# Attention in a macaron block: weighted sums turned and divided by VectorE in 32x32 blocks, and a new place for every job of the loop

## The chip, the cores and the metric

One core of a Trainium2 chip. The metric is the device time of one execution of the whole kernel in microseconds, the median of several runs. One execution was also taken by the hardware profiler; every row below is from it.

## What is computed

The input x holds 32 sequences of 256 tokens of width 128. Three residual steps follow one another:

```python
x = x + 0.5 * ffn(layernorm(x))      # shared SwiGLU + top-2 of 8 experts
x = x + attn(layernorm(x))           # causal, 16 heads of width 8
x = x + 0.5 * ffn(layernorm(x))      # the same weights again

def attn(x, W_Q, W_K, W_V, W_O):     # shapes: [32, 256, 128]
    Q, K, V = x @ W_Q.T, x @ W_K.T, x @ W_V.T      # split into 16 heads of 8
    s = where(causal, Q @ K.T / sqrt(8), -inf)
    return (softmax(s) @ V) @ W_O.T
```

The change touches the attention step alone.

## The kernel before, in words

x lies in SBUF all the time, as 64 tiles of 128 tokens. The three steps are three phases, `ffn_phase`, `attention_phase`, `ffn_phase`; each is one block in which the engines run their own instruction lists in order and meet by semaphores. Products with the weights are made of three 16-bit products (high by high, low by high, high by low), so an activation is split into a high half (a float16 copy, ScalarE) and a low half (the value minus the high half, VectorE).

`attention_phase` goes over 16 chunks of 512 tokens (two sequences, b = 0 and 1). A **turn** of the loop handles one chunk in eight **units** (b, j), j = 0 to 3; unit 0 is (0, 0), unit 4 is (1, 0). A unit is four of the 16 heads, one in each group of 32 rows. In a unit

- TensorE makes, interleaved (`both`, L1011), the key-major scores of this unit (`head_t`, L998, into three `prob` banks) and the first two of three parts of the query-major scores of the unit five ahead (`score_head`, L966, behind a causal mask that is added by a product, L956, into two `score` banks in turn). Then come the jobs of place 0, the weighing of V by the exponentials of the unit before (`weigh`, L1038, into the `o` bank), the third part of the query-major scores, and the jobs of places 1 and 2.
- VectorE takes the maxima of the three score parts (`maxima`, L1136): parts 0 and 1, then the jobs of place 0, then part 2, then the jobs of places 1 and 2. TensorE may begin a score part when the part two before it has its maximum.
- ScalarE takes the three exponentials (L1214), then the jobs of place 0, then copies the o bank of the unit before to SBUF (`take_o`, L1220), then the jobs of places 1 and 2.
- GpSimd zeroes the two causal triangles in the exponentials (L1256).

A **job** is any smaller step that passes through one of two `job` banks, which the jobs take in turn, in the order of the table PLACES (L747). TensorE writes the bank; ScalarE or VectorE or both take it; a job may begin when the one two before it has been taken. The jobs: x (turn the normalised chunk, L882; high half L1186, low half L1094), q and k (projections, L889; high halves L1189 in two halves of the rows, low halves L1098), Q00 to Q11 and K00 to K11 (place the heads for the row groups, L899; packed by VectorE at L1103 or ScalarE at L1193, L1197), v (L905, L1200), m00 to m11 (turn the negated maxima, L937; added into q's pack at L1108), o00 to o11 (turn the copied sums, L913; reciprocal L1113 and product L1115), y0 and y1 (turn y back, L922; high half L1204, low half L1121) and z0 and z1 (product with W_O; added to x at L1124). SHIFT (L754) tells for which chunk, ahead or behind, a job is done in a turn. The scores of a sequence wait for its packs Q and K of the second half (L946), the key-major products for its m jobs (L984).

The layer norm for the next chunks is spread over VectorE and GpSimd: `norm_stats` and `norm_moments` (L76, L85) at unit 5, `norm_root` on GpSimd, and `norm_scale` (L110) on VectorE at unit 6. In the feed-forward phase the scaling is done on ScalarE (L609), with `norm_shift` on GpSimd before it.

The o bank holds for each of the four groups a block of 32 rows: 8 rows of the sum, one row of the divisor (from a column of ones in `v_ones`) and 23 of zeros, over 256 queries.

Ahead of the loop one list of jobs, the maxima of the first sequence, the jobs m00, m01, x, z0, and the first maxima of the second sequence are done; behind it the last weighing and the jobs that are left.

Of the kernel before, what the change touches and what calls it, by code (L numbers as in the profile page):

```python
# [5 lines left out]
ALU = mybir.AluOpType  # L6
# [6 lines left out]
P = 128  # L13
# [12 lines left out]
MAX_ROW = 3 * HEAD  # L26
SCALE = float(HEAD) ** -0.5
# [34 lines left out]
LN_STEPS = 2 * TILES  # L62

# [654 lines left out]
def select_heads(nc, consts, done):  # L718
# [35 lines left out]
SHIFT = {n: -2 if n == "x" else -1 if n in ("m00", "m01") or n[0] in "qkQKv" else 1 if n in ("o10", "o11", "y1", "z1")  # L754
         else 0 for n in JOBS}
# [22 lines left out]
def attention_phase(nc, x, consts, w, norms):  # L778

    with ExitStack() as ctx:  # L780
# [6 lines left out]
        def sem(name):  # L787
# [19 lines left out]
        o_t = [sb(f"o_t{s}", [P, UNITS, SEQ], F32) for s in range(2)]  # L807
        inv = sb("inv", [P, 2, UNITS, GROUPS], F32)
        y = sb("y", [P, 2, P], F32)
# [10 lines left out]
        xhi_done, qkhi_done, yhi_done, inv_done = (sem(n) for n in ("xhi_done", "qkhi_done", "yhi_done", "inv_done"))  # L820
        mask_begun = sem("mask_begun")
        scored, max_done = sem("scored"), sem("max_done")
        st_done, exp_done, masked, pv_done, o_done = (
            sem(n) for n in ("st_done", "exp_done", "masked", "pv_done", "o_done"))
# [35 lines left out]
        def _(pe):  # L860
# [14 lines left out]
            def job(c, slot, name):  # L875
# [31 lines left out]
                elif kind == "o":  # L907

                    b, t = int(name[1]), int(name[2])
                    pe.wait_ge(o_done, c * 2 * UNITS + (b + 1) * UNITS)  # L910
                    dst, done = begin(c, name)
                    for j in range(UNITS):
                        last = nc.tensor.transpose(dst[:, j * P:(j + 1) * P], o_t[b][:, j, t * P:(t + 1) * P],  # L913
                                                   ident[:, :])
                elif kind == "y":
                    b = int(name[1])

                    wait_taken(pe, c, f"o{b}0")
                    wait_taken(pe, c, f"o{b}1")
                    dst, done = begin(c, name)  # L920
                    for t in range(2):
                        last = nc.tensor.transpose(dst[:, t * P:(t + 1) * P], y[:, t, :], ident[:, :])  # L922
                elif kind == "z":

                    wait_taken(pe, c, "y" + name[1])
# [100 lines left out]
            def weigh(c, slot, b, j):  # L1026
# [47 lines left out]
        def _(dve):  # L1074
# [7 lines left out]
            def scale(c):  # L1082

                wait_taken(dve, c - 1, "x")
                norm_scale(dve, nc, norm0 + c, chunk_rows(x, c), buf, ln_rooted, ln_done)

            def job(c, slot, name):
                kind = name[0]
                if kind in "Kv" or (kind == "Q" and name[2] == "1"):
                    return  # L1090
# [9 lines left out]
                elif kind == "Q":  # L1100

                    wait_count(dve, st_done, (c - 1) * 6 * UNITS)
                    last = nc.vector.tensor_copy(packed(q_pack[slot], name),  # L1103
                                                 src[:, :].rearrange("p (g n) -> p g n", n=SEQ))
# [4 lines left out]
                elif kind == "o":  # L1109

                    b, t = int(name[1]), int(name[2])
                    o = src[:, :].rearrange("p (j g r) -> p j g r", j=UNITS, r=ROWS)
                    nc.vector.reciprocal(inv[:, t, :, :], o[:, :, :, HEAD]).then_inc(inv_done, 1)  # L1113
                    dve.wait_ge(inv_done, c * 4 + 2 * b + t + 1)
                    last = nc.vector.tensor_tensor(y[:, t, :].rearrange("p (g j d) -> p j g d", j=UNITS, d=HEAD),  # L1115
                                                   o[:, :, :, 0:HEAD],
                                                   inv[:, t, :, :].unsqueeze(3).to_broadcast([P, UNITS, GROUPS, HEAD]),
                                                   ALU.mult)
                elif kind == "y":
                    dve.wait_ge(yhi_done, c * 2 + int(name[1]) + 1)  # L1120
# [222 lines left out]
```

## Time and profile before

| | us |
|---|---|
| median of 3 runs | 1214.66 |
| lowest and highest | 1207.71, 1216.27 |
| the profiled execution | 1208.36 |
| its span | 1205.8 |
| TensorE busy (matmul) | 1106.7, 92% |
| VectorE busy | 1001.9, 83% |
| ScalarE busy | 789.6, 65% |
| GpSimd busy | 562.8, 47% |

The span is from the first to the last instruction of the profiled execution. PE is TensorE's matmul, PEld its weight load, DVE VectorE, ACT ScalarE, POOL GpSimd. Busy shares are means over stages with different limits, and a matmul's duration is modelled, so it overlaps the next one's.

### The profile page before, as it was taken

To read this page: it belongs to the slowest core of one execution; us is meant where nothing else is said; L and a number is where in the kernel's file an instruction comes from. 1 tells how busy PE (TensorE), PEld (TensorE's weight loads), DVE (VectorE), ACT (ScalarE), POOL (GpSimd) and SP (SyncE) were. 2 spreads that over 40 slices of the span, in tenths; PEclk is the share of its full clock that TensorE was granted. 3 is DMA by queue.
4 is the path that set the end of the run, shared out by engine and by line. 5 is a ranking of instruction groups with operands and counts; after the bars stand their busy time and mean duration, and the time that the engine had idled before them with its cause. 6 is when DMAs were issued, how large, how long until landed. Compare 5 with 4: busy or idle time off the path is not lost. (4 is left out here: it accounts for less than half of the span.)

```text
span 1205.8 us, 31981 instructions
## 1 busy us (share of the span) xinstructions
PE 1106.7 (92%) x11588; PEld 683.5 (57%) x11588; DVE 1001.9 (83%) x2589; ACT 789.6 (65%) x1545; POOL 562.8 (47%) x722
## 2 busy tenths in 40 slices
PE   2899999999979989989999989989979999999998
PEld 1566666666525555555555555555545666666665
DVE  5889899898767888888888888888858898898985
ACT  4676767767526676676766766676646767666664
POOL 2566666666503233333333323333325666666655
PEclk9899999999968999999999999999988999999999
DMA  4442443432200000000000000000004434435333
GB/s 127 152 158 86 155 135 105 141 110 104 71 1 1 2 2 2 1 2 2 2 2 2 2 2 2 1 2 2 2 2 142 154 109 136 132 110 158 117 123 97
DMA packets 59865, 80.11 MB, mean 66 GB/s; under 512 B 5568, under 2 KB 26944, under 8 KB 59712
## 3 DMA queue, kind: packets, MB, share of 16 engines
q1 hardware_dynamic: 59712, 78.08, 20.5%
q8 instruction: 95, 1.56, 0.5%
q14 instruction: 58, 0.48, 0.1%
HBM read 73.34 MB, written 4.72 MB: 65 GB/s over the span
## 5 line engine op out<-in xcount | busy, mean ns | idle before, releaser
L696 POOL TENSOR_TENSOR h_lo<-h,h_hi 128x512 f16<-128x512 f32 x288 | 333.2, 1157 | 234.6 <-ACT h_hi L643 232.5
L1256 POOL TENSOR_SCALAR_AFFINE_SELECT probs_at<-probs_at 128x512 f32<-128x512 f32 x256 | 156.3, 634 | 343.9 <-ACT probs_at L1214 343.9
L1136 DVE TENSOR_REDUCE neg_max_at<-score_at 128x2 f16<-128x512 f32 (+1 forms) x384 | 253.9, 690 | 69.9 <-PE score_at L966 64.6
L1214 ACT ACTIVATE probs_at<-prob_at 128x512 f32<-128x512 f32 x384 | 201.7, 599 | 78.3 <-PE prob_at L998 76.4
L635 ACT ACTIVATE a<-a 128x512 f32<-128x512 f32 x256 | 149.0, 582 | 130.5 <-PE a L547 125.6
L435 DVE TENSOR_TENSOR prod<-a,gate_wide 128x512 f32<-128x512 f32 x256 | 175.9, 687 | 48.2 <-ACT a L635 46.6
L563 PE MATMUL y_b<-w_hi,h_hi 128*128 128x128 f16 x1152 | 208.2, 219 | 2.6 <-POOL h_lo L696 2.6
L563 PE MATMUL y_b<-w_lo,h_hi 128*128 128x128 f16 x1152 | 208.1, 219 | 0.0
L563 PE MATMUL y_b<-w_hi,h_lo 128*128 128x128 f16 x1152 | 208.0, 219 | 0.0
L643 ACT ACTIVATE h_hi<-h 128x512 f16<-128x512 f32 x288 | 179.5, 623 | 17.4 <-DVE h L445 16.7
L445 DVE TENSOR_TENSOR h<-prod,b 128x512 f32<-128x512 f32 x256 | 174.4, 681 | 5.3 <-issue 0.4
L956 PE MATMUL score_at<-causal,ident_b 128*128 128x256 bf16 (+1 forms) x384 | 109.2, 319 | 34.2 <-DVE neg_max_at L1136 16.2
L966 PE MATMUL score_at<-k_pack_at,q_pack_at 32*128 32x128 f16 (+1 forms) x1024 | 131.8, 248 | 0.0
L563 PEld LDWEIGHTS y_b<-w_hi,h_hi 128*128 128x128 f16 x1152 | 112.9, 98 | 29.7 <-issue 3.1
L563 PEld LDWEIGHTS y_b<-w_lo,h_hi 128*128 128x128 f16 x1152 | 112.9, 98 | 26.8
L563 PEld LDWEIGHTS y_b<-w_hi,h_lo 128*128 128x128 f16 x1152 | 112.8, 98 | 0.0
L1038 PE MATMUL o_at<-probs_at,v_ones_at 128*32 128x256 f32 (+1 forms) x2048 | 110.9, 334 | 1.7 <-POOL probs_at L1256 1.7
L547 PE MATMUL a<-xt_hi,w_hi 128*128 128x512 f16 x288 | 110.4, 383 | 0.4 <-DVE prod L435 0.4
L547 PE MATMUL a<-xt_hi,w_lo 128*128 128x512 f16 x288 | 110.4, 383 | 0.0
L547 PE MATMUL a<-xt_lo,w_hi 128*128 128x512 f16 x288 | 110.2, 383 | 0.0
L547 PE MATMUL b<-xt_hi,w_hi 128*128 128x512 f16 x288 | 109.9, 382 | 0.0
L547 PE MATMUL b<-xt_hi,w_lo 128*128 128x512 f16 x288 | 109.9, 382 | 0.0
(139 smaller groups left out, 1960.0 us busy)
## 6 DMA issues: line engine op xcount, KB each, us to landing
gate_wide<-gate_rows SPq DMA_DIRECT2D x256, 256.0 KB, 5.4
x<-in_L_attn_x_dram SPq DMA_DIRECT2D x16, 256.0 KB, 6.1
out_dram<-x SPq DMA_DIRECT2D x16, 256.0 KB, 6.9
raw_w<-in_L_ffn_w_dram SPq DMA_DIRECT2D x3, 512.0 KB, 4.9
gate_rows<-gate_rows SPq DMA_DIRECT2D x32, 16.0 KB, 1.4
raw_w<-in_L_ffn_sw_dram SPq DMA_DIRECT2D x3, 64.0 KB, 3.6
raw_attn<-in_L_attn_W_Q_dram SPq DMA_DIRECT2D x1, 64.0 KB, 4.7
raw_attn<-in_L_attn_W_K_dram SPq DMA_DIRECT2D x1, 64.0 KB, 3.5
```

The source lines that it names most:

```text
L435: nc.vector.tensor_tensor(prod[k][:, :], a_bank[k][:, :], gate_wide[c % 2][:, e - 1, :], ALU.mult).then_inc(prod_done, 1)
L445: nc.vector.tensor_tensor(h[e % 3][:, :], prod[k][:, :], b_bank[k][:, :], ALU.mult).then_inc(h_done, 1)
L547: last = nc.tensor.matmul(dst[k][:, :], ws[:, e, :], xs[s][:, :], start=(i == 0), stop=(i == 2))
L563: last = nc.tensor.matmul(y[:, tile], hs[k][:, tile], ws[:, e, :], start=(e == 0 and t == 0 and i == 0), stop=(e == STEPS - 1 and t == TIL ...
L635: nc.scalar.activation(dst[:, :], a_bank[k][:, :], ACT.Silu).then_inc(silu_done, 1)
L643: nc.scalar.activation(h_hi[k][:, :], h[k][:, :], ACT.Copy).then_inc(hhi_done, 1)
L696: nc.gpsimd.tensor_tensor(h_lo[k][:, :], h[k][:, :], h_hi[k][:, :], ALU.subtract).then_inc(hlo_done, 1)
L966: last = nc.tensor.matmul(view[:, h, :], q_pack[slot][rows, groups[h], q0:q0 + P], k_pack[slot][rows, groups[h], first:first + keys], star ...
L1038: last = nc.tensor.matmul(o_bank[g * ROWS:(g + 1) * ROWS, t * P:SEQ], v_ones[slot][:, 2 * b + t, GROUPS * g + j, :], src, start=(t == 0), ...
L1136: nc.vector.tensor_reduce(dst, src, AX.X, ALU.max, negate=True).then_inc(max_done, 1)
L1214: nc.scalar.activation(probs[j % 2][:, i, :], prob_bank[i][:, :], ACT.Exp, scale=SCALE).then_inc(exp_done, 1)
L1256: nc.gpsimd.affine_select(out=p, in_=p, compare_op=ALU.is_ge, fill=0.0, base=0, pattern=[[0, GROUPS], [1, P]], channel_multiplier=-1).then ...
```

## The change

1. The jobs o and y are gone. The o bank now holds two units side by side in its 32 rows (each head of a pair has 16: 8 sums, the divisor, zeros; the other 16 columns of its weights are zeros, so that both accumulate), and the second pair lies in the second half of the bank, so that the bank is full after the four units of a sequence. `divide` on VectorE, in units 0 and 4, then does four steps: step 0 turns the bank in 32x32 blocks into SBUF, ahead of the third maximum of the unit; step 1 takes the reciprocals; step 2 multiplies; step 3 turns the result back. `split_y` on ScalarE (units 1 and 5) makes the high half, `low_y` on GpSimd the low half, and z begins when `ylo_done` says so. `take_o` is gone.
2. The layer norm's scaling is on ScalarE, half at the end of unit 3 and half at the end of unit 4; moments, root and a new shift are at unit 2.
3. All four Q packs are on ScalarE.
4. PLACES is new: q is made two chunks ahead, in unit 6, k in unit 1, both in place 0, x in place 0 of unit 5.
5. Ahead of the loop the jobs are put between the first maxima.

```diff
+OUT_ROWS = ROWS // 2
+O_STEPS = 4
...
-PLACES = (((), ("q",), ("k",)), (("o10",), ("o11",), ("Q00",)), (("K00",), ("Q01",), ("K01",)),
-          (("m10", "m11"), ("y1",), ()),
-          (("z1",), ("Q10",), ("K10",)), (("o00",), ("o01",), ("Q11",)), (("K11",), ("y0",), ("v",)),
-          (("m00", "m01"), ("x",), ("z0",)))
+PLACES = (((), ("Q00",), ("Q01",)), (("k",), (), ()), (("K00",), ("K01",), ("z1",)), (("m10", "m11"), ("v",), ()),
+          ((), ("Q10",), ("Q11",)), (("x",), (), ("K10",)), (("q",), ("K11",), ("z0",)), (("m00", "m01"), (), ()))
...
+SHIFT = {n: -2 if n in "xq" else -1 if n in ("m00", "m01") or n[0] in "qkQKv" else 1 if n == "z1" else 0 for n in JOBS}
+BESIDE_FIRST = [JOBS.index(n) for n in ("z1", "Q10", "x", "q", "m00")]
...
+        def v_places(slot):
+            return v_ones[slot][:, :, :, :].rearrange("p t (n i) (k r) -> p (t n) (i k) r", i=2, r=OUT_ROWS)
+
+        def last_weighed(do, c, b, j):
+            if j == 0 and b == 1:
+                do(c, 0)
+            elif j == 0 and exists(c - 1):
+                do(c - 1, 1)
...
                 elif kind == "z":
-                    wait_taken(pe, c, "y" + name[1])
+                    pe.wait_ge(ylo_done, 2 * c + int(name[1]) + 1)
...
                 pe.wait_ge(masked, unit * 2 + 2)
-                wait_count(pe, o_done, unit)
+                if j == 0:
+                    wait_count(pe, o_step, (2 * c + b - 1) * O_STEPS + 1)
...
-                        last = nc.tensor.matmul(o_bank[g * ROWS:(g + 1) * ROWS, t * P:SEQ],
+                        pair = slice(j // 2 * SEQ + t * P, (j // 2 + 1) * SEQ)
+                        last = nc.tensor.matmul(o_bank[g * ROWS:(g + 1) * ROWS, pair],
                                                 v_ones[slot][:, 2 * b + t, GROUPS * g + j, :], src,
-                                                start=(t == 0), stop=(t == 1), skip_group_check=True)
+                                                start=(t == 0 and j % 2 == 0), stop=(t == 1 and j % 2 == 1),
+                                                skip_group_check=True)
...
-            turn_jobs(job, -1, 1, JOBS[:-4])
+            turn_jobs(job, -2, 0, JOBS)
+            turn_jobs(job, -1, 1, JOBS[:BESIDE_FIRST[0]])
             for j in range(UNITS):
                 scores(0, 0, 0, j)
-            turn_jobs(job, -1, 1, JOBS[-4:])
+                turn_jobs(job, -1, 1, JOBS[BESIDE_FIRST[j]:BESIDE_FIRST[j + 1]])
+            turn_jobs(job, -1, 1, JOBS[BESIDE_FIRST[UNITS]:])
...
+            def divide(c, b, step):
+                n = 2 * c + b
+                if step > 0:
+                    dve.wait_ge(o_step, n * O_STEPS + step)
+                if step == 0:
+                    dve.wait_ge(pv_done, (n + 1) * UNITS)
+                    done = nc.vector.transpose(o_rows[:, :, :, :].rearrange("p n i r -> p (n i r)"), o_bank[:, :])
+                elif step == 1:
+                    done = nc.vector.reciprocal(inv[:, :, :], o_rows[:, :, :, HEAD])
+                elif step == 2:
+                    done = nc.vector.tensor_tensor(y[:, :, :, :].rearrange("p s n (i d) -> p (s n) i d", d=HEAD),
+                                                   o_rows[:, :, :, 0:HEAD],
+                                                   inv[:, :, :].unsqueeze(3).to_broadcast(
+                                                       [P, 2 * SEQ // ROWS, 2, HEAD]), ALU.mult)
+                else:
+                    wait_count(dve, ylo_done, n)
+                    done = nc.vector.transpose(yt[:, :], y[:, :, :, :].rearrange("p s n r -> p n s r"))
+                done.then_inc(o_step, 1)
...
                         if ahead:
                             maxima(ahead[0], *ahead[2:], parts=(0, 1))
                         turn_jobs(job, c, slot, places[0])
+                        last_weighed(lambda *seq: divide(*seq, 0), c, b, j)
                         if ahead:
                             maxima(ahead[0], *ahead[2:], parts=(2,))
+                        last_weighed(lambda *seq: divide(*seq, 1), c, b, j)
                         turn_jobs(job, c, slot, places[1])
-                        if b == 1 and j == 1:
+                        last_weighed(lambda *seq: divide(*seq, 2), c, b, j)
+                        if b == 0 and j == 2:
                             norm(c + 2)
-                        if b == 1 and j == 2:
-                            scale(c + 2)
                         turn_jobs(job, c, slot, places[2])
+                        last_weighed(lambda *seq: divide(*seq, 3), c, b, j)
...
+            def scale(c, tiles):
+                act.wait_ge(shifted, 2 * (c - 2) + 2)
+                wait_taken(act, c - 1, "x")
+                for t in tiles:
+                    last = nc.scalar.activation(xn[:, t, :], chunk_rows(x, c)(t), ACT.Identity,
+                                                scale=buf["rstd"][:, t:t + 1], bias=buf["shift"][:, t:t + 1])
+                if t == TILES - 1:
+                    last.then_inc(ln_done, 1)
+
+            def split_y(c, b):
+                act.wait_ge(o_step, (2 * c + b + 1) * O_STEPS)
+                if b == 1:
+                    wait_taken(act, c, "z0")
+                elif not is_first(c):
+                    wait_taken(act, c - 1, "z1")
+                nc.scalar.activation(yt_hi[:, :], yt[:, :], ACT.Copy).then_inc(yhi_done, 1)
...
                         turn_jobs(job, c, slot, places[0])
-                        if j > 0:
-                            take_o(c, b, j - 1)
-                        elif b == 1:
-                            take_o(c, 0, UNITS - 1)
-                        elif exists(c - 1):
-                            take_o(c - 1, 1, UNITS - 1)
+                        last_weighed(split_y, c, b, j - 1)
                         turn_jobs(job, c, slot, places[1])
                         turn_jobs(job, c, slot, places[2])
+                        if b == 0 and j == 3:
+                            scale(c + 2, range(2))
+                        if b == 1 and j == 0:
+                            scale(c + 2, range(2, TILES))
...
+            def low_y(c, b):
+                pool.wait_ge(yhi_done, 2 * c + b + 1)
+                nc.gpsimd.tensor_tensor(yt_lo[:, :], yt[:, :], yt_hi[:, :], ALU.subtract).then_inc(ylo_done, 1)
...
                         mask(c, b, j)
-                        if b == 1 and j == 1:
+                        last_weighed(low_y, c, b, j - 1)
+                        if b == 0 and j == 2:
                             norm_root(pool, nc, norm0 + c + 2, buf, ln_step, ln_rooted)
+                            norm_shift(pool, nc, c, norm0 + c + 2, buf, ln_rooted, shifted)
```

## Rows read from the trace of the kernel before

Columns of a timeline row: start in us from the span's start, duration in us, engine, line, operation, output<-input, shapes, how many; in brackets the idle time before it and what ended it. A row with x2 or more merges instructions in a row.

**Rows 1.** Windows: stretch; busy us of PE, PEld, DVE, ACT, POOL; clock, DMA, GB/s.
```profile
342.00:860.00 518.00, 470.29 (x5516) 271.55 (x5518) 423.45 (x906) 349.30 (x692) 162.91 (x268) 0.98 0.01 2
```

**Rows 2.** Timeline of TensorE: first key-major product of nine units.
```profile
599.58 0.28 PE L998 MATMUL prob_at<-q_pack_at,k_pack_at 32*128 32x256 f16 x1
...
604.90 0.28 PE L998 MATMUL prob_at<-q_pack_at,k_pack_at 32*128 32x256 f16 x1
...
609.43 0.28 PE L998 MATMUL prob_at<-q_pack_at,k_pack_at 32*128 32x256 f16 x1
...
613.26 0.28 PE L998 MATMUL prob_at<-q_pack_at,k_pack_at 32*128 32x256 f16 x1
...
616.86 0.28 PE L998 MATMUL prob_at<-q_pack_at,k_pack_at 32*128 32x256 f16 x1
...
620.66 0.28 PE L998 MATMUL prob_at<-q_pack_at,k_pack_at 32*128 32x256 f16 x1
...
624.55 0.28 PE L998 MATMUL prob_at<-q_pack_at,k_pack_at 32*128 32x256 f16 x1
...
628.94 0.28 PE L998 MATMUL prob_at<-q_pack_at,k_pack_at 32*128 32x256 f16 x1
...
632.90 0.28 PE L998 MATMUL prob_at<-q_pack_at,k_pack_at 32*128 32x256 f16 x1
```

**Rows 3.** Timelines of ScalarE, VectorE and TensorE in units 2 to 4.
```profile
605.33 1.57 ACT L1214 ACTIVATE probs_at<-prob_at 128x512 f32<-128x512 f32 x3 [2.30 <-PE prob_at L998]
...
606.77 0.70 ACT L1197 ACTIVATE k_pack_at<-job_at,max_row 128x512 f16<-128x512 f32 x1
...
609.90 1.29 DVE L1136 TENSOR_REDUCE neg_max_at<-score_at 128x4 f16<-128x512 f32 x2 [1.78 <-PE score_at L966]
...
611.10 1.28 DVE L1108 TENSOR_TENSOR q_pack_at<-job_at,q_pack_at 128x512 f16<-128x512 f32 x2
...
615.25 0.28 PE L956 MATMUL score_at<-causal,ident_b 128*128 128x256 bf16 x1
...
615.89 0.70 DVE L1136 TENSOR_REDUCE neg_max_at<-score_at 128x2 f16<-128x512 f32 x1 [0.55 <-PE score_at L966]
```

**Rows 4.** Timelines of ScalarE and VectorE: low halves of q, then maxima.
```profile
632.03 1.21 ACT L1189 ACTIVATE q_stack_at<-job_at 64x512 f16<-64x512 f32 x2 [0.81 <-PE job_at L870]
...
632.72 1.39 DVE L1098 TENSOR_TENSOR q_stack_at<-job_at,q_stack_at 64x512 f16<-64x512 f32 x2 [0.75 <-ACT q_stack_at L1189]
...
635.57 0.70 DVE L1136 TENSOR_REDUCE neg_max_at<-score_at 128x4 f16<-128x512 f32 x1
```

**Rows 5.** Groups by line and form: count; busy us, mean ns; idle us before.
```profile
L1103 DVE CAST q_pack_at<-job_at 128x512 f16<-128x512 f32 x32 | 21.8, 680 | 2.2 <-PE job_at L899 2.1
...
L372 DVE RECIPROCAL below<-below 128x32 f32<-128x32 f32 x32 | 11.3, 353 | 1.1
...
L913 PE MATMUL job_at<-ident,o_t_at 128*128 128x128 f32 x204 | 33.1, 285 | 6.9 <-DVE q_stack_at L1098 6.9
```

**Rows 6.** Timeline of ScalarE in the first feed-forward stage.
```profile
105.42 0.87 ACT L609 ACTIVATE xn<-x,shift,rstd 128x128 f32<-128x128 f32 x2
...
106.19 0.62 ACT L643 ACTIVATE h_hi<-h 128x512 f16<-128x512 f32 x1
```

**Rows 7.** Timelines of ScalarE, TensorE and VectorE: a pack's end; moments.
```profile
608.23 0.68 ACT L1197 ACTIVATE k_pack_at<-job_at,max_row 128x512 f16<-128x512 f32 x1
...
609.01 0.48 PE L956 MATMUL score_at<-causal,ident_b 128*128 128x512 bf16 x2 [1.01 <-ACT q_pack_at L1193]
...
620.73 0.86 DVE L76 BATCH_NORM_STATS2 stats<-x 128x6 f32<-128x128 f32 x4
...
621.93 2.06 DVE L1136 TENSOR_REDUCE neg_max_at<-score_at 128x4 f16<-128x512 f32 x3
```

**Rows 8.** Windows before the loop: stretch; PE busy us (count), granted clock, DMA, GB/s.
```profile
345.10:348.50 3.40, 2.88 (x19) 1.00 0.00 0
...
348.50:351.90 3.40, 3.40 (x14) 0.50 0.02 5
```

More of the change, by code:

```diff
@@ L806, in attention_phase @@
         probs = [sb(f"probs{s}", [P, 3, CHUNK], F32) for s in range(2)]
-        o_t = [sb(f"o_t{s}", [P, UNITS, SEQ], F32) for s in range(2)]
-        inv = sb("inv", [P, 2, UNITS, GROUPS], F32)
-        y = sb("y", [P, 2, P], F32)
+        o_rows = sb("o_rows", [P, 2 * SEQ // ROWS, 2, OUT_ROWS], F32)
+        inv = sb("inv", [P, 2 * SEQ // ROWS, 2], F32)
+        y = sb("y", [P, 2, SEQ // ROWS, OUT_ROWS], F32)
+        yt = sb("yt", [P, SEQ], F32)
         yt_hi, yt_lo = sb("yt_hi", [P, SEQ], F16), sb("yt_lo", [P, SEQ], F16)
@@ L819, in attention_phase @@
         buffers_set = sem("buffers_set")
-        xhi_done, qkhi_done, yhi_done, inv_done = (sem(n) for n in ("xhi_done", "qkhi_done", "yhi_done", "inv_done"))
-        mask_begun = sem("mask_begun")
+        xhi_done, qkhi_done, yhi_done, ylo_done = (sem(n) for n in ("xhi_done", "qkhi_done", "yhi_done", "ylo_done"))
+        mask_begun, shifted = sem("mask_begun"), sem("shifted")
         scored, max_done = sem("scored"), sem("max_done")
-        st_done, exp_done, masked, pv_done, o_done = (
-            sem(n) for n in ("st_done", "exp_done", "masked", "pv_done", "o_done"))
+        st_done, exp_done, masked, pv_done, o_step = (
+            sem(n) for n in ("st_done", "exp_done", "masked", "pv_done", "o_step"))
         block = ctx.enter_context(nc.Block())
@@ L906, in job @@
                                                       (xt_lo[:, tile], w_hi[:, 2, :])))
[L907 to L922, printed above, removed]
                 elif kind == "z":
-                    wait_taken(pe, c, "y" + name[1])
+                    pe.wait_ge(ylo_done, 2 * c + int(name[1]) + 1)
                     dst, done = begin(c, name)
@@ L1080, in norm @@
                 norm_moments(dve, nc, norm0 + c, buf, ln_step)
-            def scale(c):
-                wait_taken(dve, c - 1, "x")
-                norm_scale(dve, nc, norm0 + c, chunk_rows(x, c), buf, ln_rooted, ln_done)
             def job(c, slot, name):
                 kind = name[0]
-                if kind in "Kv" or (kind == "Q" and name[2] == "1"):
+                if kind in "QKv":
                     return
@@ L1099, in job @@
                                                        stack[kind][half][rows, :], ALU.subtract)
[L1100 to L1104, printed above, removed]
                 elif kind == "m":
@@ L1108, in job @@
                     last = nc.vector.tensor_tensor(q, src[:, :].rearrange("p (g q) -> p g q", q=P), q, ALU.add)
[L1109 to L1120, printed above, removed]
-                    last = nc.vector.tensor_tensor(yt_lo[:, :], src[:, 0:SEQ], yt_hi[:, :], ALU.subtract)
                 elif kind == "z":
@@ L1165, in _ @@
                 maxima(0, 0, j)
-            turn_jobs(job, -1, 1, JOBS[-4:])
+                turn_jobs(job, -1, 1, JOBS[BESIDE_FIRST[j]:BESIDE_FIRST[j + 1]])
+            turn_jobs(job, -1, 1, JOBS[BESIDE_FIRST[UNITS]:])
             maxima(0, 1, 0)
             run_chunks(turn)
+            for step in range(O_STEPS):
+                divide(CHUNKS - 1, 1, step)
             turn_jobs(job, CHUNKS, 0, JOBS)
@@ L1174, in job @@
                 kind = name[0]
-                if kind in "moz" or (kind == "Q" and name[2] == "0"):
+                if kind in "mz":
                     return
-                if kind == "y":
-                    b = int(name[1])
-                    if b == 1:
-                        wait_taken(act, c, "z0")
-                    elif not is_first(c):
-                        wait_taken(act, c - 1, "z1")
                 src, done = take(act, c, name)
@@ L1215, in exponents @@
                                          scale=SCALE).then_inc(exp_done, 1)
-            def take_o(c, b, j):
-                unit = c * 2 * UNITS + b * UNITS + j
-                act.wait_ge(pv_done, unit + 1)
-                nc.scalar.activation(o_t[b][:, j, :], o_bank[:, 0:SEQ], ACT.Copy).then_inc(o_done, 1)
             def turn(c, slot):
```

23 lines of the change are left out of this document (12 added, 11 removed).

## The prediction

> **What bounds the kernel now.** I read the windows by stage first: the attention stage is 518 us of the 1205.8 us span, TensorE is busy for 470 of them, VectorE for 423, ScalarE for 349 [rows 1]. The two feed-forward stages are not edited; the case is the attention loop, 16 turns (one chunk each) of eight units. No engine is full there, so I went on to the timeline of one turn. It repeats to a few hundredths: the units start at the times of [rows 2], which hold units 1 to 7 of one turn and 0 and 1 of the next, and last 3.96 (unit 0), 5.32, 4.53, 3.83, 3.60, 3.80, 3.89 and 4.39 us, 33.32 in all.
>
> A unit begins with the interleaved key-major and score products. Units 2 to 4 show the skeleton [rows 3], with T a unit's start: at T+0.43 the three exponentials begin (1.57 us; ScalarE's next instruction starts 1.44 after their start); at T+0.47 VectorE takes two maxima, and its next instruction starts 1.20 later; TensorE weighs the unit before, then makes the third part of the scores, whose mask starts at T+1.99 in unit 4. 0.44 of that is the job z1 in front (counting its gap); without a job it is T+1.55. The third maximum follows 0.64 later. Call its start M: the next unit starts 0.97 after it (615.89 to 616.86), because the second mask needs its bank. So a unit lasts M+0.97 unless TensorE or a pack is later, M is T+2.19 at the earliest, and **whatever stands in VectorE's queue ahead of the third maximum, which is place 0 of a unit, lengthens the unit**; places 1 and 2 are mostly covered. Unit 1 is the longest because the low halves of q and k are in VectorE's queue in front of its maxima, which come at T+2.67 instead of T+0.47 [rows 2, 4].
>
> **The change by its parts.**
> *Turning the sums.* Gone per turn: 20 TensorE transposes, four o jobs of four (285 ns each, pipelined to some 0.6 a job [rows 5]) and two y jobs of two, some 2.9 us of TensorE; eight copies of ScalarE; four reciprocals and multiplies of VectorE. Added on VectorE for each of two sequences: a block transpose of 128x512 from PSUM, a reciprocal of 32, a multiply of 256, a block transpose of 256. The trace shows no block transpose. The nearest row is the cast 128x512 out of PSUM, 680 ns, some 0.60 to the next start as with the maxima [rows 3, 5]; I take that. Bounds: 0.35, the reciprocal of 32, and twice the cast, 1.2. The rest is 0.35 for the reciprocal [rows 5] and, between the two rows, 0.42 each for the 256-wide operations, 1.2 in all. Step 0 stands before the third maximum and waits for the weighing, which ends at T+1.62: it starts at T+1.70 and M becomes 2.30. Units 0 and 4: **3.27** each (before 3.96 and 3.60). The other three steps end at T+4.1 and delay the next maxima by 0.3, which units 1 and 5 cover (below). If the step takes 1.2, both units get 0.6 longer.
>
> The Trainium skill, "VectorE: DVE Perf Modes", The three transpose paths, calls the 32x32 turn VectorE's fastest within a bank and gives 311 ns for 128x128 bf16; no row here shows one. Scaling that at one column a cycle gives an estimate of about 0.7 us for 512, and the sum would not move.
>
> *k, q and x go to place 0.* This is the part that speaks against the change. In place 0 ScalarE does the high halves right after its exponentials, from T+1.86; VectorE's first low half starts 0.69 after the high one, the two take 1.39 and the next instruction can follow 0.03 later: 2.11 after the high half began [rows 4]. So M=T+1.86+2.11=T+3.97 and **units 1 and 6 last 4.94** (before 5.32 and 3.89). VectorE waits idle from T+1.67 to T+2.55 and the third maximum is queued behind it; TensorE, done with the scores at T+2.8, waits for that. q and k no longer share one unit, but each now pays its full chain. K11 on ScalarE (ends T+3.8) and z0 on TensorE (waits for q's bank until T+4.0) are just covered.
> Unit 5 has x in place 0. The scaling now on ScalarE decides here: two of its 128x128 take 0.87, 0.77 to the next start, in the feed-forward stage [rows 6]. In unit 3, v is ready at T+3.5, scaling ends the unit 0.8 into unit 4; in unit 4, Q10, Q11 (0.49 apart, ready at T+2.52) and two more scalings hold ScalarE to T+4.27, 1.0 into unit 5. Its exponentials start 0.58 late, x's high half starts at T+2.44, its low half 0.69 later, as q's does [rows 4], and 0.61 after that M=T+3.74, say 3.75: **4.72** (before 3.80).
> The skill's same page, The TRN2 errata, says small operands read from SBUF pay a fixed extra cost per instruction; its 224+128 cycles would be 0.29 us each, the trace has 0.385 from start to start. By the page's figure unit 5 would be 0.2 shorter.
>
> *Units 2, 3, 7.* Unit 2: K00 in place 0, K01 in place 1. K01 is written on TensorE at about T+2.8 and packed by ScalarE until T+3.53; scores of the next chunk wait for it, and the unit follows 0.52 after a pack's end (608.91 to 609.43) [rows 2, 7]: **4.05** (before 4.53, with three packs in it). The moments move here, 1.20 us on VectorE [rows 7], after the third maximum, and z1 behind them; they push unit 3's maxima 0.14 late. Unit 3: two additions, 1.28 us or 1.20 to the next start [rows 3], before the third maximum, as now, v on TensorE covered: **3.98** (3.83). Unit 7: x, z0 and the scaling are gone, it becomes what unit 3 is now: **3.84** (4.39).
> GpSimd gets two low halves (half of a 128x512, some 0.6 us each) and two tiny operations. Both low halves end over 2 us before z needs them; the unit's masks come 0.5 late once, and the weighing that needs them is 1.3 away. I cost them at nothing.
> The two Q casts leave VectorE for ScalarE in units 0 and 4, where ScalarE has room; cost only the share in unit 5 above.
>
> Sum of a turn: 3.27+4.94+4.05+3.98+3.27+4.72+4.94+3.84 = 33.01 against 33.32: **0.3 us less, 5 us over 16 turns**. TensorE loses 2.9 us of work a turn and gets nearly all of it back as waiting. Entry and exit: before the loop q, x and the second pair of packs now lie between the first maxima, where TensorE and not VectorE is late, and q of chunk 1 is added there; I estimate 4 us more. At the exit turn 14 has no q (1.3 less) and the last chunk has no o and y jobs (2.5 less). I take 0, bounds 5 either way. The profiled execution took 1208.36 us, so it would take about 1203; the median of the runs shown is 6.3 above it, so on the scale of the runs I give 1214.66-5 = 1210.
>
> **Rivals.**
> *Loads decide, not chains.* If the waits I put in place 0 overlap better than I think, the turn follows the loads: TensorE loses 2.9 and VectorE about 2 of work. For: the old turn is 1.1 times the sum of its busiest engines' unit loads, and the new placing spreads these evenly. Against: VectorE takes strictly in order and unit 1 shows today what that costs [rows 2, 4]. Half of the relief, 1.5 a turn, is -24: 1190.
> *The clock falls.* The granted clock was 1.00 from 345.10 to 348.50, with TensorE at short score products and waits of 0.3 us, and 0.50 right after (the higher and the lower of its levels, 2.4 and 1.2 GHz) [rows 8]; over the whole stage its mean is 0.98 [rows 1], so the loop keeps the higher one. Units 1 and 6 now have TensorE idle for almost 2 us on end, more than the 1.01 that is the most in today's turn [rows 7]: 32 such places. In each where the clock falls, products and weighing on the chain (0.76, 0.79 and 0.3 us) take twice as long, some 1.9 us. Nine falls cancel 5 us of gain and pass 1% slower; 16 give +30-5: 1240.
> *The block transpose is dear.* At twice the cast, 0.6 x 2 x 16 = +19, with the rest as forecast: 1229. It decides from about 1.15 us. If transpose, reciprocal and multiply all double, unit 1 still covers the tail.
> *Nothing is removed*: not open; the o and y jobs are not in the new list.
>
> **How the numbers follow.** About 1% is what a measurement of this kernel can tell from no change. Forecast (within 1%): 0.50. Loads decide: 0.27, faster. Clock: 0.12, transpose: 0.11, both slower. Range 1188 to 1234: it takes in the transpose's upper bound and most of the first rival, and leaves out the clock falling at every other place. The forecast's own range is 1200 to 1221.
>
> **What would show it.** Right: unit starts 33.0 apart per turn; third maxima of units 1 and 6 near T+4.0 with 0.9 us of VectorE waiting for the high halves before them; xt_hi starting 2.4 into its unit; the block transpose 0.6 to 0.7 us; PE busy in the stage down by some 35 us and its waits for the maxima up by as much. Wrong: a turn under 32, a granted clock below 0.95 in the loop, a 128x512 transpose above 1 us, or an entry that takes over 8 us more.

## The result: 2.7% slower, and where the time is in the profile after

The changed kernel takes 1246.45 us (median of 4; 1240.36 to 1251.46) against 1215.47 for the kernel before, run beside it: ratio 1.0268, 95% interval 1.0218 to 1.0318 (the medians by themselves give 1.0255). Ratios here leave out executions over 1.5% above the fastest of their kernel. The profiled execution took 1242.78 us, its span is 1240.9, 35.1 more than before. The forecast was 1210.

The page of the kernel after: busy time by engine, and the granted clock in 40 slices of 31 us.

```profile
PE 1115.0 (90%) x11268; PEld 669.9 (54%) x11268; DVE 981.4 (79%) x2463; ACT 782.0 (63%) x1513; POOL 592.6 (48%) x786
...
PEclk9899999999859899899798978989968999999999
```

VectorE and ScalarE are busy for 20.5 and 7.6 us less, as the diff says, but TensorE, which lost 20 transposes a turn, is busy for 8.3 us **more**. The clock row explains it: over the loop it dips again and again, and its mean over the span is 0.931, before 0.977. Windows of the kernel after, columns as in [rows 1]: the attention stage, an undisturbed turn, one with a small dip, one of the two longest turns.

```profile
342.00:900.00 558.00, 484.42 (x5299) 262.20 (x5301) 412.74 (x801) 346.65 (x671) 191.81 (x331) 0.89 0.01 2
...
687.88:720.97 33.09, 28.14 (x348) 15.62 (x348) 26.43 (x52) 22.62 (x44) 12.75 (x22) 1.00 0.01 2
617.08:651.06 33.98, 29.40 (x347) 16.21 (x347) 26.42 (x52) 22.62 (x44) 12.75 (x22) 0.95 0.01 2
720.97:760.45 39.48, 35.13 (x348) 18.79 (x348) 26.80 (x52) 22.62 (x44) 12.74 (x22) 0.78 0.00 1
```

Instructions and the other engines' work are the same in the three turns; TensorE's busy time is 28.14, 29.40 and 35.13 us, the clock 1.00, 0.95 and 0.78, the length 33.09, 33.98 and 39.48. With the clock held a turn is 33.09 us, which answers to the 33.32 of [rows 2] and is what the walk forecast (33.01). Now the place where a dip begins, in the turn of 617.08, and the same place of the undisturbed turn (the last two lines; the two turns start 70.80 us apart, and so do the windows).

```profile
617.00:620.34 3.34, 3.21 (x41) 1.76 (x41) 2.77 (x5) 2.32 (x5) 1.23 (x2) 1.00 0.00 0
620.34:623.00 2.66, 2.66 (x37) 1.46 (x36) 2.15 (x5) 2.55 (x6) 0.99 (x2) 1.00 0.03 9
623.00:626.50 3.50, 1.98 (x24) 1.06 (x26) 2.72 (x5) 1.61 (x4) 0.90 (x2) 1.00 0.00 0
626.50:630.00 3.50, 3.35 (x27) 1.55 (x24) 1.82 (x5) 2.06 (x4) 1.23 (x2) 0.51 0.00 0
630.00:634.00 4.00, 3.97 (x56) 2.56 (x56) 3.96 (x13) 1.61 (x4) 2.86 (x6) 1.00 0.00 0
...
693.80:697.30 3.50, 1.99 (x24) 1.06 (x26) 2.72 (x5) 1.61 (x4) 0.91 (x2) 1.00 0.02 5
697.30:700.80 3.50, 3.09 (x43) 1.73 (x40) 2.68 (x12) 2.30 (x5) 1.31 (x3) 1.00 0.02 5
```

In unit 1 TensorE is busy for 1.98 of 3.50 us while it waits for the third maximum; right behind it the clock stands at its lower level (0.51, 1.2 GHz) for 3.4 us, and TensorE gets through 27 instructions in those 3.50 us, against 43 in the same stretch of the undisturbed turn. The same wait there has 1.99 of 3.50 in front of it and no dip behind. In the kernel before, the thinnest stretch of that length in a turn is this one (window of the kernel before), and its longest wait on TensorE is 1.01 [rows 7]:

```profile
600.00:603.50 3.50, 2.32 (x31) 1.26 (x27) 3.41 (x7) 2.98 (x6) 1.08 (x2) 1.00 0.00 0
```

The 3.5 us are my choice, one length for all kernels; what stretch the chip looks at is not known from these runs.

**The 35.1 us.** The loop begins at 368.18, before at 362.29: +5.9. The first 15 turns take 528.45 us, before 500.61: +27.8. At the undisturbed length they would be 15 x 33.09 = 496.35, 4.3 **less** than before; turn 14 without q is 1.25 shorter, one turn 0.35 longer, and the disturbed turns add the rest, 33.0: 1.6 in turn 0, and 31.4 in twelve dips of turns 1 to 13 (3.7, 1.0, 0.9, 3.7, 6.4 for two, 0.9, 3.7, 6.4 for two, 1.0, 3.7), 2.6 us each. From the last turn to the end it is 344.3, before 342.9: +1.4, and in its last units the clock is low too.

The new operations cost what was taken for them. Groups of the kernel after, 400 to 880 us, columns as in [rows 5], and VectorE's timeline at the start of the undisturbed turn.

```profile
L1207 ACT ACTIVATE xn<-x,shift,rstd 128x128 f32<-128x128 f32 x52 | 22.6, 486 | 0.0
L1113 DVE STREAM_TRANSPOSE o_rows_at<-o_at 128x512 f32<-128x512 f32 x27 | 19.4, 717 | 0.0
L1271 POOL TENSOR_TENSOR yt_lo_at<-yt_at,yt_hi_at 128x256 f16<-128x256 f32 x27 | 18.1, 670 | 9.9 <-ACT yt_hi_at L1219 9.9
L1123 DVE STREAM_TRANSPOSE yt_at<-y_at 128x256 f32<-128x256 f32 x27 | 12.0, 445 | 0.9
```

```profile
688.35 1.29 DVE L1134 TENSOR_REDUCE neg_max_at<-score_at 128x4 f16<-128x512 f32 x2 [0.74 <-PE score_at L962]
689.57 0.72 DVE L1113 STREAM_TRANSPOSE o_rows_at<-o_at 128x512 f32<-128x512 f32 x1
690.21 0.66 DVE L1134 TENSOR_REDUCE neg_max_at<-score_at 128x2 f16<-128x512 f32 x1
690.78 0.33 DVE L1115 RECIPROCAL inv_at<-o_rows_at 128x32 f32<-128x32 f32 x1
691.15 0.42 DVE L1117 TENSOR_TENSOR y_at<-o_rows_at,inv_at 128x256 f32<-128x256 f32 x1
691.61 0.45 DVE L1123 STREAM_TRANSPOSE yt_at<-y_at 128x256 f32<-128x256 f32 x1
691.98 1.26 DVE L1134 TENSOR_REDUCE neg_max_at<-score_at 128x4 f16<-128x512 f32 x2
693.71 1.39 DVE L1094 TENSOR_TENSOR k_stack_at<-job_at,k_stack_at 64x512 f16<-64x512 f32 x2 [0.47 <-ACT k_stack_at L1187]
695.13 0.70 DVE L1134 TENSOR_REDUCE neg_max_at<-score_at 128x2 f16<-128x512 f32 x1
```

The block transpose of 128x512 out of PSUM holds VectorE for 0.64 us (689.57 to 690.21), taken 0.60. The Trainium skill, "VectorE: DVE Perf Modes", The three transpose paths, led by scaling to an estimate of 0.7 us; the trace's duration, 0.717, agrees.

TensorE's timeline behind these maxima is the chain to which the forecast put its walk:

```profile
693.98 0.39 PE L952 MATMUL score_at<-causal,ident_b 128*128 128x512 bf16 x1
695.88 0.28 PE L952 MATMUL score_at<-causal,ident_b 128*128 128x256 bf16 x1 [1.51 <-DVE neg_max_at L1134]
696.10 0.28 PE L994 MATMUL prob_at<-q_pack_at,k_pack_at 32*128 32x256 f16 x1
```

Unit 1 starts at 691.14, its third maximum at T+3.99 (forecast 3.97), the next unit 0.97 later. This wait of TensorE, 1.51 us, is the longest of the turn; over the loop the longest is 1.52.

### The profile page after: what moved, and what is told of

It is laid out like the page before. It is cut to its first block and busy times, and to the rows that moved or that the text cites. A ratio compares the mean times of both kernels' runs of the same rounds, so it can differ in the third digit from the quotient of the medians.

```text
span 1240.9 us, 31083 instructions
## 1 busy us (share of the span) xinstructions
PE 1115.0 (90%) x11268; PEld 669.9 (54%) x11268; DVE 981.4 (79%) x2463; ACT 782.0 (63%) x1513; POOL 592.6 (48%) x786
## 3 DMA queue, kind: packets, MB, share of 16 engines
q8 instruction: 92, 1.51, 0.5%
HBM read 73.34 MB, written 4.72 MB: 63 GB/s over the span
## 5 line engine op out<-in xcount | busy, mean ns | idle before, releaser
L952 PE MATMUL score_at<-causal,ident_b 128*128 128x256 bf16 (+1 forms) x384 | 124.7, 339 | 53.8 <-DVE neg_max_at L1134 43.6
L962 PE MATMUL score_at<-k_pack_at,q_pack_at 32*128 32x128 f16 (+1 forms) x1024 | 140.6, 259 | 0.0
L1036 PE MATMUL o_at<-probs_at,v_ones_at 128*32 128x256 f32 (+1 forms) x2048 | 124.6, 367 | 1.0 <-POOL probs_at L1266 1.0
L994 PE MATMUL prob_at<-q_pack_at,k_pack_at 32*128 32x256 f16 (+1 forms) x1024 | 114.7, 255 | 0.0
```

Source lines behind the costliest of these rows:

```text
L952: nc.tensor.matmul(view[:, :, keys - P:keys], consts["ident_b"][:, :], consts["causal"][:, :].unsqueeze(1).to_broadcast([P, len(groups), P ...
L962: last = nc.tensor.matmul(view[:, h, :], q_pack[slot][rows, groups[h], q0:q0 + P], k_pack[slot][rows, groups[h], first:first + keys], star ...
```

## The experiments

All ratios are to the kernel before, run beside each. Two theories stood against each other: the 30 us are the clock, which falls because TensorE has too little to do in the places with waits; or the chains and the entry are dearer than the walk says.

**The clock held, nothing else changed.** The kernel after, with products that change nothing (the causal mask's product, repeated into the score bank of the next unit's first part, which that unit's own mask overwrites with `start=True`) in the waits of units 1 and 6:

```diff
+FILL = {(0, 1): 6, (1, 2): 4}
...
+            def fill(c, slot, b, j):
...
+                    for _ in range(count):
+                        wait_count(pe, max_done, later * 24 + later_b * 12 + 3 * later_j - 1)
+                        nc.tensor.matmul(score_bank[3 * later_j % 2][:, :].rearrange("p (h k) -> p h k", k=P),
+                                         consts["ident_b"][:, :],
+                                         consts["causal"][:, :].unsqueeze(1).to_broadcast([P, GROUPS, P]),
+                                         start=True, stop=True, skip_group_check=True)
```

> The changed kernel with idempotent extra products on TensorE in its two long waits: after place 1 of unit 1 six, and of unit 6 four more copies of the causal mask's product (128x512, about 0.215 us each at the higher clock) into the score bank that the next unit's own mask overwrites anyway. Nothing is left out. Theory (the clock): in the changed kernel ten turns out of fifteen contain a stretch at a granted clock of 0.5; the shortest turns, untouched by it, last 33.1 us and the disturbed ones 34.0 to 39.5. If TensorE's waits are what lets the clock fall, every turn comes to 33.1 to 33.3 and the time falls by about 30 us, to 1215 to 1220. Rival (the fall has another cause, such as the power or the mix of work): the clock falls as often, and the turns get longer, by what the extra products cost: 1246 to 1260.

Measured: 1212.23 us, ratio 1.0001 (0.998 to 1.0023), a little under what the theory of the clock gave. Windows of this kernel: the place in unit 1, a turn, and the loop.

```profile
607.80:611.30 3.50, 3.28 (x30) 1.60 (x32) 2.71 (x5) 1.61 (x4) 0.87 (x2) 1.00 0.00 0
403.40:436.40 33.00, 30.21 (x357) 16.48 (x356) 26.42 (x52) 22.61 (x44) 12.72 (x22) 1.00 0.01 2
365.00:885.00 520.00, 475.03 (x5528) 258.34 (x5526) 407.51 (x806) 349.81 (x683) 200.29 (x347) 0.99 0.01 2
```

Ten more products a turn, 34 us less. From 377 to 882 us, inside the last turn, no dip is left; turns 1 to 12 are 33.08 long, their units as in the undisturbed turn of the kernel after within 0.02. So the clock is the whole of the loop's loss. With it held the change is worth nothing as a whole: the first 15 turns take 497.76, 2.9 less than before, but the loop begins at 368.04, 5.7 later, and from the last turn to the end it is 344.7, 1.8 more; both of these places are still at the low level in part.

**Two products in unit 1 alone** (`FILL = {(0, 1): 2}`).

> The same with two extra products, in unit 1 only. Theory: a smaller dose removes a part of the slow stretches, unit 6 keeps its own; 1225 to 1242. Rival: as the changed kernel, 1246, since two products of 0.2 us change nothing.

Measured: 1222.37 us, ratio 1.0086 (1.0057 to 1.0116). That is just under the range that was expected, and far from the rival. The low stretches inside the loop sum to 51.7 us, in the kernel after to 106.3, in the kernel with ten products to 14.1. Some 60% of what the ten products remove is gone from the low time, and 24 of their 34 us from the loss: the loss goes roughly by how much low clock there is.

**The turning and dividing alone**, in the kernel before: its places less the jobs o and y, its norm, its Q packs and its entry.

```diff
-PLACES = (((), ("q",), ("k",)), (("o10",), ("o11",), ("Q00",)), (("K00",), ("Q01",), ("K01",)),
-          (("m10", "m11"), ("y1",), ()),
-          (("z1",), ("Q10",), ("K10",)), (("o00",), ("o01",), ("Q11",)), (("K11",), ("y0",), ("v",)),
-          (("m00", "m01"), ("x",), ("z0",)))
+PLACES = (((), ("q",), ("k",)), ((), (), ("Q00",)), (("K00",), ("Q01",), ("K01",)), (("m10", "m11"), (), ()),
+          (("z1",), ("Q10",), ("K10",)), ((), (), ("Q11",)), (("K11",), (), ("v",)), (("m00", "m01"), ("x",), ("z0",)))
```

> The kernel before with the turning and dividing on VectorE alone: the places of the old list less the o and y jobs (z1 stays in unit 4, x and z0 in unit 7), the old division of the Q packs, the old norm and scaling, the old entry. Theory (chains in place 0 decide, turning is nearly free): unit 0 stays at 4.0, unit 1 grows to 5.5 to 5.7 because divide stands with q and k on VectorE, units 2 and 5 lose 0.3 each, so a turn is 33.1 and the time about 1212 if the clock holds; it may fall in the long unit 1. Rival (TensorE's load is what counts): 2.9 us less of TensorE's work a turn, 1175 to 1190. Second rival (the turning itself is the loss): 1235 or more with the granted clock at 1.00 in the loop.

Measured: ratio 1.0722 (1.0643 to 1.0801), the slowest of all, and neither theory had it. Three executions took 1291.31 to 1309.55 us, at a mean clock of 0.875 to 0.859 over the span; the fourth, 1345.73 us at 0.822, is the one that was profiled, so the rows show the loss larger than the ratio does. Windows of one turn, of 100 us, and two around a fall, then TensorE's timeline there:

```profile
443.90:489.40 45.50, 41.28 (x349) 21.42 (x350) 29.04 (x58) 20.47 (x38) 12.25 (x20) 0.62 0.00 1
400.00:500.00 100.00, 88.50 (x806) 45.94 (x806) 69.85 (x137) 48.17 (x90) 28.83 (x47) 0.70 0.01 1
...
619.50:623.00 3.50, 0.76 (x17) 0.31 (x9) 3.36 (x7) 2.52 (x5) 1.67 (x3) 1.00 0.01 2
623.00:626.50 3.50, 3.25 (x27) 1.66 (x29) 2.92 (x5) 1.33 (x3) 0.30 (x2) 0.65 0.00 0
```

```profile
622.81 0.28 PE L951 MATMUL score_at<-causal,ident_b 128*128 128x256 bf16 x1 [2.74 <-DVE neg_max_at L1139]
```

The clock is at 0.70 over the 100 us, some two and a half turns. With the old places the low halves of q and k stand in VectorE's queue ahead of the maxima of unit 1 [rows 4], and the transposes were what TensorE did meanwhile; without them it waits for 2.74 us on end and is busy for 0.76 of 3.50, and the clock falls there in each of the turns. The thinnest stretch is 2.32 in the kernel before, 1.98 in the kernel after, 0.76 here, and the three stand in the same order in their clock and time (other kernels here do not keep to this order, see **Open** below). So the new places, which I had called the adverse part of the change, are kinder to the clock than the old ones with the transposes merely taken out.

**The same with the clock held** (products into a `prob` bank that has been read, 10, 4, 2 and 1 of them in units 1, 2, 3 and 4, 17 a turn):

> The kernel with the turning alone (old places less o and y) with extra mask products (128x512) on TensorE into a score-transposed bank that is free by then: ten in unit 1 between the weighing and the third part of the scores, four at the end of unit 2, two of unit 3, one of unit 4. Without them it was 1302 us, at a granted clock of 0.65 to 0.70 in the loop; its units without a slow stretch were 3.96 (0), 3.2 (5), 3.5 (6) and 4.0 us (7), shorter than or equal to those of the kernel before. Theory: what made it slow is the clock alone, and it fell since TensorE lost the turning of o and y; with the waits filled a turn is 32.0 to 33.0, and the time 1190 to 1210, below the kernel before. Rival: VectorE's queue in units 0 and 1 (divide beside q and k) is what costs; then the loop stays above 35 us a turn at a clock of 1.00, and the time above 1240.

```profile
431.80:465.00 33.20, 31.29 (x364) 17.13 (x363) 28.44 (x58) 20.48 (x38) 12.25 (x20) 1.00 0.01 2
```

Measured: 1208.3 us, ratio 0.9968 (0.9944 to 0.9992). Window of one turn above: clock 1.00, 33.20 us. Some 90 us of the kernel of the last experiment were the clock (the mean of its three shorter executions is 1298.8); what the turning itself does to a turn, with these products in it, is 33.32 to 33.2, and not the 32.0 to 33.0 that were expected.

**The old entry** in the kernel after (all the jobs before the first maxima in one list):

```diff
-            turn_jobs(job, -1, 1, JOBS[:BESIDE_FIRST[0]])
+            turn_jobs(job, -1, 1, JOBS[:BESIDE_FIRST[UNITS]])
...
-                turn_jobs(job, -1, 1, JOBS[BESIDE_FIRST[j]:BESIDE_FIRST[j + 1]])
```

> The changed kernel with its jobs ahead of the loop as one list before the first maxima, as in the kernel before, not between them. Theory: the entry of the changed kernel costs 6 us more than before (its loop begins at 368.2 against 362.3 us) since all its extra products stand in TensorE's queue at the lower clock; in one list the jobs go one after the other through two banks, so this is no better: the loop begins 2 us earlier to 3 us later, and the time moves by under 5 us, plus or minus what the slow stretches do in the loop (their position shifts). Rival: the interleaving costs the 6 us, and the time falls by them.

Measured: 1246.8 us, ratio 1.0301 (1.0268 to 1.0335). The loop begins at 367.36, only 0.8 earlier: the order of the jobs is not what the entry lost. The dips in the loop lie at other times than in the kernel after and sum to more (122.6 us at the low level, against 106.3); the first 15 turns take 534.64, 6.2 more, which is why the earlier start doesn't show in the time. The clock of this entry is low too, so what the added job q costs there by itself is not separated.

**The entry with the clock held** (the first experiment, with further products: 26 before the job list, 9 behind k, 4 behind K01, one with each of the first score groups).

> The changed kernel with filled waits (1212 us), and the waits ahead of the loop filled too: 26 extra products while the buffers are set, nine after k, four after K01, one after each group of first scores. The stretch from 332 to 376 us has a granted clock of 0.50. Theory: with the clock held, TensorE's products ahead of the loop take half; the loop begins 3 to 6 us earlier and its first units lose 3: 1203 to 1207. Rival: the entry waits for ScalarE and VectorE, and the time stays within 2 us of 1212; or the clock falls there all the same.

Windows of the entry, first of the kernel after, then of this one, then two of the kernel before:

```profile
332.00:348.00 16.00, 6.70 (x26) 2.28 (x26) 7.67 (x14) 4.72 (x8) 0.00 (x0) 0.53 0.00 0
348.00:362.00 14.00, 13.53 (x60) 5.76 (x57) 7.71 (x12) 3.70 (x7) 0.00 (x0) 0.50 0.01 1
362.00:376.00 14.00, 12.38 (x77) 5.82 (x77) 8.22 (x13) 7.56 (x13) 2.46 (x4) 0.50 0.00 0
```

```profile
332.00:348.00 16.00, 14.12 (x82) 6.34 (x81) 8.63 (x16) 5.31 (x9) 0.00 (x0) 1.00 0.00 1
348.00:362.00 14.00, 9.98 (x63) 4.42 (x61) 10.06 (x16) 5.41 (x8) 0.00 (x0) 0.90 0.00 0
362.00:376.00 14.00, 14.00 (x103) 6.46 (x102) 6.66 (x10) 7.34 (x14) 3.13 (x6) 0.61 0.01 2
```

```profile
332.00:348.00 16.00, 9.01 (x46) 3.61 (x47) 8.84 (x15) 6.85 (x11) 0.00 (x0) 0.68 0.00 0
348.00:362.00 14.00, 12.14 (x52) 4.60 (x50) 9.76 (x15) 1.88 (x2) 0.00 (x0) 0.52 0.00 1
```

Measured: 1207.25 us, ratio 0.9958 (0.9932 to 0.9985). In the kernel after the entry runs at the low level throughout, from 348 to 362 with TensorE busy for 13.53 of 14 us. Held high up to 359.2, the loop begins at 362.07, 6.0 earlier than in the first experiment; then the clock is low for 13.7 us, and turn 0 gives 0.9 back.

**The same products in the entry of the kernel before** (24 behind k, 3 behind Q00, one with each group):

> The kernel before with extra products ahead of its loop only (24 after k, three after Q00, one after each group of first scores). Theory: the clock ahead of the loop is worth several us to either kernel and has nothing to do with the change; in the changed kernel filling it gave 5 us, here 2 to 5 us: 1206 to 1210. Rival: the kernel before has nothing to gain there, 1211 to 1213.

Measured: 1211.75 us, ratio 1.0003 (0.9976 to 1.003): the 2 to 5 us that were expected did not come. The loop begins at 363.06, 0.8 later than without. The clock is 0.89 from 332 to 348, in the job list, where it was 0.68, and 0.52 from 348 to 362, as without. Why the products hold the clock through one entry and not through the other was not tried.

The trace of this kernel shows one thing more. Its loop is that of the kernel before, unedited, and there the clock falls once, in turn 12, which takes 36.05 us:

```profile
768.20:771.70 3.50, 2.32 (x30) 1.24 (x27) 3.42 (x6) 2.84 (x6) 1.22 (x2) 1.00 0.02 5
771.70:778.50 6.80, 6.80 (x47) 3.58 (x47) 3.91 (x9) 2.53 (x5) 1.23 (x3) 0.50 0.00 0
```

So the old loop is not free of falls. The executions of the kernel before, beside the first experiment, go from 1207.40 us at a mean clock of 0.974 to 1218.42 at 0.964.

**k later.** With the clock held, is the long unit 1 k's chain ahead of the third maximum? The first experiment, with k in place 1 behind it and two products in unit 2 instead of six in unit 1:

```diff
-FILL = {(0, 1): 6, (1, 2): 4}
+FILL = {(0, 2): 2, (1, 2): 4}
...
-PLACES = (((), ("Q00",), ("Q01",)), (("k",), (), ()), (("K00",), ("K01",), ("z1",)), (("m10", "m11"), ("v",), ()),
+PLACES = (((), ("Q00",), ("Q01",)), ((), ("k",), ()), ((), ("K00",), ("K01", "z1")), (("m10", "m11"), ("v",), ()),
```

> The changed kernel with filled waits (1212 us, 33.08 a turn), and k moved from place 0 to place 1 of unit 1, K00 to place 1 and K01 to place 2 of unit 2. Theory (place 0 chains the unit through ScalarE's exponentials and both halves of k): unit 1 falls from 4.96 to about 3.2, unit 2 grows from 4.05 to 4.3 to 4.6, unit 3 to 4.1 to 4.5 (VectorE is later with the moments): a turn of 32.0 to 32.3, time 1195 to 1200. Rival (VectorE's load per pair of units is what counts, the place is not): units 1 to 3 together stay at 13.07 and the time at 1212.

Measured: 1203.85 us, ratio 0.9931 (0.9901 to 0.996); the turn is 32.48 (expected 1195 to 1200, and 32.0 to 32.3). Unit 1 goes from 4.96 to 3.17, unit 2 from 4.04 to 5.47 and unit 3 from 4.07 to 3.83. Timeline of TensorE and VectorE in its unit 2:

```profile
604.46 1.39 DVE L1110 TENSOR_TENSOR k_stack_at<-job_at,k_stack_at 64x512 f16<-64x512 f32 x2 [0.75 <-ACT k_stack_at L1203]
605.88 1.29 DVE L1150 TENSOR_REDUCE neg_max_at<-score_at 128x4 f16<-128x512 f32 x2
...
606.63 0.28 PE L953 MATMUL score_at<-causal,ident_b 128*128 128x256 bf16 x1 [1.03 <-DVE neg_max_at L1150]
```

The chain leaves unit 1 as expected but k's low halves now stand ahead of unit 2's first maxima, and the third part of the scores waits for those (1.03). Of the 1.8 us gained in unit 1, 0.6 stay, a third.

**The scaling on VectorE**, at the end of unit 3, with the clock held:

```diff
+                        if b == 0 and j == 3:
+                            wait_taken(dve, c + 1, "x")
+                            norm_scale(dve, nc, norm0 + c + 2, chunk_rows(x, c + 2), buf, ln_rooted, ln_done)
...
-                        if b == 0 and j == 3:
-                            scale(c + 2, range(2))
-                        if b == 1 and j == 0:
-                            scale(c + 2, range(2, TILES))
```

> The changed kernel with filled waits (1212 us), and the scaling back on VectorE, at the end of unit 3. Theory (ScalarE's scaling makes unit 5 late through the exponentials): unit 5 falls from 4.71 to about 4.15, unit 4 grows from 3.26 to about 3.55 since its maxima start later on VectorE: 0.25 to 0.35 less a turn, 1207 to 1209. Rival: ScalarE's lateness in unit 5 is covered, unit 5 stays at 4.7 and the turn gets 0.3 longer: 1217.

Measured: 1206.78 us, ratio 0.9933 (0.9905 to 0.9961); the turn is 32.68. Unit 5 goes from 4.71 to 4.16 and unit 4 from 3.26 to 3.42: 0.55 of unit 5 was the scaling ahead of its exponentials (forecast 0.58).

**The filled entry, k later and the scaling on VectorE together.**

> The changed kernel with all that helped put together: filled waits in the loop and ahead of it, k in place 1 of unit 1 (K00 and K01 in places 1 and 2 of unit 2), the scaling on VectorE at the end of unit 3. Theory (the gains stand in different units): a turn is 32.48 less 0.40, 32.1 us; the loop begins 5 us earlier than at 367.5; the time is 1190 to 1196, 1.3 to 1.8% below the kernel before. Rival (they share VectorE's slack around units 3 and 4): a turn of 32.5, 1198 to 1202.

```profile
434.00:466.10 32.10, 29.05 (x355) 16.30 (x354) 27.42 (x56) 21.41 (x40) 12.28 (x20) 1.00 0.01 2
```

Measured: 1195.01 us (1193.34 to 1196.8), ratio 0.9853 (0.9824 to 0.9883): faster than both kernels, 1.5% under the one and 4% under the other. A turn (above, the window of one) is 32.08, the loop begins at 362.08; turn 0 takes 38.7 at a low clock and two more are 33.2, so it is not all held.

## Why the prediction was wrong

**The walk of the turn held.** Units of the undisturbed turn against the forecast, us:

| unit | 0 | 1 | 2 | 3 | 4 | 5 | 6 | 7 | sum |
|---|---|---|---|---|---|---|---|---|---|
| forecast | 3.27 | 4.94 | 4.05 | 3.98 | 3.27 | 4.72 | 4.94 | 3.84 | 33.01 |
| measured | 3.26 | 4.96 | 4.04 | 4.07 | 3.25 | 4.72 | 4.96 | 3.83 | 33.09 |

The block transpose, the chains of k and q in place 0, the scaling's delay of unit 5 and the covers of unit 2 are each within 0.1. The rival that loads decide falls with the same table, the one of the dear transpose with its 0.64.

**The entry** was forecast at +4 and is +5.9. Its stated reason, more jobs between the first maxima, is not borne out: with the old order it is 0.8 less. With the clock held it is gone (362.07 against 362.29), but the kernel before is itself at 0.68 and 0.52 there, so this doesn't compare the two at one clock. The forecast had entry and exit together at 0, bounds 5 either way; they are 5.9-1.25+1.4, some 6. **The exit** was forecast at -3.8 (1.3 and 2.5). The 1.3 came (turn 14: -1.25), the 2.5 turned into +1.4, in units at a low clock; what of it is the clock alone was not tried.

**The step that failed** is "over the whole stage its mean is 0.98 [rows 1], so the loop keeps the higher one", that is the clock counted as held and its rival put at 0.12. The mechanism, the places (units 1 and 6, TensorE waiting for the third maximum) and a price of 1.9 us a fall stood in the rival: twelve falls and turn 0, against 32 places, made 33 us. The twelve cost 2.6 each and not 1.9, because they are not alike: five of the low stretches last 3.4 us and cost 0.9 to 1.0 each, the other seven last 10.2 or 13.7 us. Ten of the falls come at the end of unit 1 or in the first 1.5 us of unit 2, behind the wait of unit 1, and two (612.9 and 756.2) 0.8 to 0.9 us into unit 7, behind that of unit 6. Nine were enough to pass 1% and 1240 was named for 16. The mean of the old loop spoke of the old loop, with 20 more transposes a turn and no wait over 1.02; the forecast itself had TensorE lose 2.9 us of work a turn and get "nearly all of it back as waiting", and that waiting, and not only its longest piece, should have been put beside the clock. [rows 8] showed one fall behind a window with 2.88 of 3.40 busy, fuller than what the new unit 1 holds at its wait (1.98 of 3.50); it pointed the right way and was weighed too lightly.

**Open.** Why the same wait brings a fall in one turn and none two turns later was not settled; the falls move when the entry is edited. How thin the thinnest 3.50 us are does not foretell it either. The kernel with k later has 2.14 in each of turns 1 to 14 (first line) and no fall in them; the one with two products has 2.42 in most, and falls eight times in its 15 turns (the next two lines, one of them):

```profile
508.10:511.60 3.50, 2.14 (x20) 1.09 (x16) 3.30 (x11) 2.38 (x5) 1.22 (x2) 1.00 0.00 0
...
613.30:616.80 3.50, 2.42 (x24) 1.19 (x23) 2.51 (x4) 1.59 (x4) 1.20 (x2) 1.00 0.01 2
616.90:620.30 3.40, 3.40 (x29) 1.67 (x27) 1.58 (x4) 1.89 (x5) 1.22 (x2) 0.50 0.00 0
```

What is shown is that more products in the waits hold the clock, not how many are needed.

## What to carry to other kernels

Work taken off TensorE is worth nothing where another engine's chain sets the unit, and can cost the clock of all that is left: read the granted clock turn by turn, not as a mean, and ask what it does when the waits grow. Products that change nothing, in the waits, tell in one run what of a loss is the clock. Then shorten the waits: only with the clock held do the real differences between two orders show (here 1.0%, from 1207.25 to 1195.01, both with the loop and the entry filled).

## What the hardware did that was not expected

- The clock fell with TensorE never idle for more than 1.52 us on end, behind 3.50 us in which it was busy for 1.98; it didn't behind another 3.50 with 1.99. In other kernels it fell behind 2.32 and 2.42, and held through 14 turns with 2.14 in each.
- The kernel with 20 transposes a turn taken out and the old places kept took 1291 to 1346 us; 17 products a turn that compute nothing brought it to 1208.3.
- A busy TensorE doesn't say that its clock is up: from 348 to 362 it was busy for 13.53 of 14.00 us at 0.50.
